# Turning the softmax maxima of each attention head: one VectorE block transpose and four ScalarE copies instead of four TensorE transposes and one copy

## The reference, cut to what matters

```python
y_dca, y_main = y[:, -16:, :], y[:, :-16, :]
q = _ln((x @ Wq + bq).reshape(b, s1, H, HD), qn_w, qn_b)      # H = 16, HD = 32
k, v = _ln(key half of y_main, kn_w, kn_b), value half of y_main
ctx = softmax(q k^T * HD ** -0.5) v
ctx = ctx + softmax(q k_dca^T * HD ** -0.5) v_dca
x = x + ctx @ Wo + bo
# then layer norm, a router with the top 6 of 64 experts, SwiGLU experts, a shared expert
```

## Time and profile before

| | |
|---|---|
| median of three runs | 1738.54 us (1735.64, 1738.54, 1740.47) |
| profiled execution, own time | 1737.14 us |
| its span | 1735.4 us |
| TensorE busy (matmul) | 1675.9 us, 97% of the span, 11782 instructions |
| VectorE busy | 1089.4 us, 63%, 2159 instructions |
| ScalarE busy | 1030.7 us, 59%, 1875 instructions |
| GpSimd busy | 769.1 us, 44%, 719 instructions |
| heads stage | about 77 to 600 us of the span |

### The profile page before, as it was taken

How to read it: one execution, slowest core, us unless ns; L and a number is a source line. 1 busy time by engine, 2 the same in 40 slices (tenths; PEclk the granted TensorE clock), 3 DMA queues, 4 the chain that set the end, 5 groups by cost and what they waited for, 6 DMA issues and landing times.

```text
span 1735.4 us, 35874 instructions
## 1 busy us (share of the span) xinstructions
PE 1675.9 (97%) x11782; PEld 1534.1 (88%) x11782; DVE 1089.4 (63%) x2159; ACT 1030.7 (59%) x1875; POOL 769.1 (44%) x719
## 2 busy tenths in 40 slices
PE   4799999999999999999999999999999999999996
PEld 3588888888888889999999999999999999999995
DVE  7555656777677665434666666666666666666665
ACT  4567766666646452223666666666666666666665
POOL 6523222334323330351355555555555555555554
PEclk9999999999999999999999999999999999999998
DMA  5543433433322532313577777778777777777775
GB/s 191 169 118 88 126 101 98 122 84 104 94 81 80 180 110 100 112 38 128 184 220 214 219 230 220 208 213 228 225 211 206 225 225 214 215 223 220 227 210 168
DMA packets 148634, 287.71 MB, mean 166 GB/s; under 512 B 29230, under 2 KB 66350, under 8 KB 139328
## 3 DMA queue, kind: packets, MB, share of 16 engines
q1 hardware_dynamic: 115584, 236.05, 42.0%
q0 software_dynamic: 32960, 50.51, 14.0%
HBM read 241.83 MB, written 64.52 MB: 177 GB/s over the span
## 4 chain that ended last, share of the span: by engine, by line
PE 88%; ACT 3%; issue 3%; DVE 2%; POOL 1%; DMA 1%; POOLq 1%; DVEq 0%; ACTq 0%; SPq 0%
PE ps L2490 37%; PE ps L2508 19%; PE ps L1470 8%; PE ps L1478 5%; PE ps L1451 4%; PE ps L2467 4%; PE ps L1441 3%; PE ps L1467 2%; PE ps L1493 2%; PE ps L1426 1%; PE ps L2485 1%; PE ps L2831 1%; ACT prob L1138 1%; DMA raw_gu<-in_w_gu 1%; ACT L1138 0%
## 5 line engine op out<-in xcount | busy, mean ns | idle before, releaser
L2217 POOL DMA_INDIRECT out<-y,ids_s x128 | 206.5, 1613 | 301.8 <-issue 162.6
L2490 PE MATMUL ps<-xt_hi,gu_hi 128*128 128x256 f32 (+1 forms) x1856 | 303.0, 285 | 0.6 <-issue 0.6
L2490 PE MATMUL ps<-xt_lo,gu_hi 128*128 128x256 f32 (+1 forms) x1856 | 290.3, 278 | 0.0
L2490 PE MATMUL ps<-xt_hi,gu_lo 128*128 128x256 f32 (+1 forms) x1856 | 289.6, 278 | 0.0
L2256 DVE TENSOR_TENSOR gu_lo<-raw_gu,gu_hi 128x1408 fp32r<-128x1408 f32 (+2 forms) x132 | 214.6, 1626 | 112.4 <-ACT gu_hi L2253 112.3
L1138 ACT ACTIVATE prob<-ps 128x512 f32<-128x512 f32 x256 | 152.3, 597 | 183.0 <-PE ps L1451 180.4
L2490 PEld LDWEIGHTS ps<-xt_hi,gu_hi 128*128 128x128 f32 (+1 forms) x1856 | 251.4, 181 | 7.6 <-issue 0.9
L2490 PEld LDWEIGHTS ps<-xt_lo,gu_hi 128*128 128x128 f32 (+1 forms) x1856 | 244.7, 181 | 0.0
L2490 PEld LDWEIGHTS ps<-xt_hi,gu_lo 128*128 128x128 f32 (+1 forms) x1856 | 244.6, 181 | 0.0
L2197 POOL DMA_INDIRECT xg<-h_rows,ids_g x128 | 189.4, 1480 | 114.3 <-POOL ids_g L2192 50.6
L2313 ACT ACTIVATE h_hi<-h 128x256 fp32r<-128x256 f32 (+1 forms) x240 | 100.5, 419 | 222.0 <-DVE h L2382 221.9
(11 more groups left out here) (318 smaller groups left out, 3001.3 us busy)
## 6 DMA issues: line engine op xcount, KB each, us to landing
raw_gu<-in_w_gu SPq DMA_DIRECT2D x70, 1408.0 KB, 8.4
raw_d<-in_w_d SPq DMA_DIRECT2D x70, 512.0 KB, 4.1
raw_d<-in_w_d SPq DMA_DIRECT2D x70, 192.0 KB, 4.5
qs<-qk_rows SPq DMA_DIRECT2D x192, 64.0 KB, 2.0
ks<-qk_rows SPq DMA_DIRECT2D x192, 64.0 KB, 2.0
xa<-in_x SPq DMA_DIRECT2D x16, 256.0 KB, 2.9
qk_rows<-k_hi SPq DMA_DIRECT2D x16, 256.0 KB, 2.2
qk_rows<-k_lo SPq DMA_DIRECT2D x16, 256.0 KB, 2.5
```

Of the source, the lines that this page charges most:

```text
L2217: pool.indirect_dma_start(out=out, out_offset=bass.IndirectOffsetOnAxis(B.ids_s[:, p, k:k + 1], 0), in_=B.y[:, p, k, :], in_offset=None, b ...
L2490: last = pe.matmul(gu_banks(it, c)[half], gu_columns(w, it, half, d, c), x[:, x_p, d, 0:W], start=i == 0, stop=i == len(steps) - 1)
```

## The change

Before, the maxima of a head were turned by four transposes on TensorE into PSUM, and ScalarE copied 32 rows of 512 out of PSUM. Now VectorE runs one transpose instruction on the whole of `nmax` behind the maxima of a head's second half (`turn_maxima`). It transposes each 32 x 32 block in place of the block, so that in the new tile `turned_max` the rows of tokens 32a to 32a + 31 of every token tile lie on partitions 32a to 32a + 31. ScalarE gathers them with four copies, one from each group of 32 partitions, each of 32 rows by four pieces of 32 tokens, out of SBUF into `qs[96:128]`. The wait of `turn_scores(n, 0)` is for the last of the four. The four transposes of `opened(n)` go, with their waits, among them those for the router's use of the bank TRB.

```diff
+            def turn_maxima(n):
+                if not head(n):
+                    return
+                if n >= 1:
+                    dve.wait_ge(shift_ready.sem, shift_ready.value(n - 1, 1))
+                dve.transpose(turned_max[:], nmax[:, n % 2].bitcast(F32).rearrange("p t j -> p (t j)")).then_inc(turned_ready.sem, 1)
...
                 maxima(n + 1, 1)
+                turn_maxima(n + 1)
...
             def shift_rows(n):
                 if not head(n):
                     return
-                act.wait_ge(nmT_ready.sem, nmT_ready.value(n, 1))
-                act.activation(qs[96:128, n % RING, :], ps[0:32, TRB, :], ACT.Copy).then_inc(nmT_in.sem, 1)
+                act.wait_ge(turned_ready.sem, turned_ready.value(n, 1))
+                rows = qs[96:128, n % RING, :].rearrange("p (t a j) -> p t a j", t=T, j=32)
+                for a in range(P // 32):
+                    last = act.activation(rows[:, :, a, :],
+                                          turned_max[32 * a:32 * a + 32, :].rearrange("p (t j) -> p t j", j=32), ACT.Copy)
+                last.then_inc(shift_ready.sem, 1)
...
-            def shift_turned(n):
...
-                pe.wait_ge(nmax_ready.sem, nmax_ready.value(n, 2))
-                if n >= 1:
-                    pe.wait_ge(nmT_in.sem, nmT_in.value(n - 1, 1))
...
-                for t in range(T):
-                    last = pe.transpose(ps[0:32, TRB, t * P:(t + 1) * P], nmax[:, n % 2, t, :].bitcast(F32), ident[:])
-                last.then_inc(nmT_ready.sem, 1)
...
                 if c == 0:
-                    pe.wait_ge(nmT_in.sem, nmT_in.value(n, 1))
+                    pe.wait_ge(shift_ready.sem, shift_ready.value(n, 1))
...
             def opened(n):
-                shift_turned(n)
                 scores(n + 1, 0)
```

More of the change, by code:

```diff
@@ L154, in attention_phase @@
         prob = sb("prob", [P, 2, T, S])
-        nmax = sb("nmax", [P, 2, T, 32], F32R)
+        nmax, turned_max = sb("nmax", [P, 2, T, 32], F32R), sb("turned_max", [P, T * 32])
         rz = sb("rz", [P, T, 2])
@@ L219, in attention_phase @@
         score_ready, nmax_ready = sig("score_ready", 2), sig("nmax_ready", 2)
-        nmT_ready, nmT_in = sig("nmT_ready", 1), sig("nmT_in", 1)
+        turned_ready, shift_ready = sig("turned_ready", 1), sig("shift_ready", 1)
         sT_ready, prob_ready = sig("sT_ready", T), sig("prob_ready", T)
@@ L657, in maxima @@
                 dve.wait_ge(score_ready.sem, score_ready.value(n, half + 1))
-                if half == 0 and n >= 2:
-                    dve.wait_ge(nmT_ready.sem, nmT_ready.value(n - 2, 1))
                 t = slice(2 * half, 2 * half + 2)
@@ L932, in front @@
                     maxima(0, 1)
+                    turn_maxima(0)
             front_begin()
@@ L954, in heads_vector @@
                 maxima(n + 2, 1)
+                turn_maxima(n + 2)
                 if projects:
@@ L966, in heads_vector @@
                 maxima(n + 3, 1)
+                turn_maxima(n + 3)
                 take_pos(u - 6)
@@ L977, in heads_vector @@
                 maxima(n + 4, 1)
+                turn_maxima(n + 4)
                 if projects:
@@ L1413, in heads_tensor @@
         def heads_tensor(pe, net):
-            def shift_turned(n):
-                if not head(n):
-                    return
-                pe.wait_ge(nmax_ready.sem, nmax_ready.value(n, 2))
-                if n >= 1:
-                    pe.wait_ge(nmT_in.sem, nmT_in.value(n - 1, 1))
[L1420 to L1424, removed]
-                for t in range(T):
-                    last = pe.transpose(ps[0:32, TRB, t * P:(t + 1) * P], nmax[:, n % 2, t, :].bitcast(F32), ident[:])
-                last.then_inc(nmT_ready.sem, 1)
             def scores(n, half):
@@ L1781, in heads_tensor @@
             wo_half(WAIT1, 1)
-            pe.wait_ge(nmT_in.sem, nmT_in.value(HEADS - 1, 1))
             a_last(WAIT1 + 2, pos_taken, GROUP1 - 1)
```

## The result

The changed kernel takes 1846.57 us (median of four runs, 1837.61 to 1847.51) where the kernel before takes 1738.99 us beside it: a ratio of 1.061, 95% interval 1.0574 to 1.0646. It is slower by 6%, about 108 us, ten times the 11 us that were forecast and far outside the range. The direction was right; the size was not.

What follows compares the result with a forecast made beforehand. TensorE was taken to bound the heads stage, already waiting for ScalarE at some points. The profiled 1737.1 us + 7.9 for heads + 3 for the clock = 1748.0; the median lies 1.4 above, so 1749 us, range 1734 to 1758.

Steps and rivals of the forecast that it cites:

- What bounds the kernel: Heads stage: TensorE bounds it as a whole, busy 512.29 of 524.00 us, but already stands idle for ScalarE at some points.
- The prices: Per head: four ScalarE copies cost 0.64 us more, TensorE saves 0.36 us, VectorE's transpose takes 0.40 us at most, hidden.
- The first rival: ScalarE's four copies overlap, costing 0.29 us more per head instead of 0.64: about 1735.5 us; chance 0.18.
- The second: Only TensorE's busy time counts, so all 23 us of transposes are saved: about 1716 us; chance 0.05.
- The heads: Gains and losses summed over all kinds of heads: 5.8 us gained, 13.7 lost, 7.9 us slower.
- the cover: Time hiding VectorE's transpose behind other work; if gone in three fourth heads that wait for VectorE's division, 1.2 us.
- The clock: Late third heads: more TensorE idle time makes two more of six fall to 1.2 GHz, 3 us, between 0 and about 7.
- The third rival: The clock falls in most late heads, 10 × 1.4 = 14 us on top: about 1758 us; chance 0.15.

Runs made afterwards that it cites:

- kernel with filler: The changed kernel with unneeded transposes of a constant on TensorE at openings that wait and ahead of waiting turns of scores; 1749.15 us, ratio 1.0068.

## Why the prediction was wrong, point by point

**What bounds the kernel** was right: TensorE as a whole, ScalarE at the openings.

**The prices** were right. The turn on ScalarE costs 0.67 us more (0.64 forecast), the transpose on VectorE 0.31 us and hidden (0.40 at the most). The first rival, overlapping copies, is out: 1.26 us from the first to the end of the fourth. The second, 23 us saved whole, is out too.

**The heads** were nearly right: 11.5 us where 7.9 were forecast. In the kernel with filler the clock stays up, and the time from the fourth exponential of one head to that of the next, less the same in the kernel before, can be summed by kind (us, worked out from the starts of L1138 and L1152):

| heads | forecast | kernel with filler |
|---|---|---|
| 10 third, query product | −3.6 | −4.0 |
| 7 fourth, key product | −1.7 | −1.5 |
| 3 fourth, wait for VectorE | 0 | +1.2 |
| 10 first, wo_product | 0 | +0.5 |
| head 20 and heads 0, 1 | −0.5 | −0.2 |
| 6 second, a_turned (units 4 to 9) | +1.1 | +1.2 |
| 8 with a plain opening (7 early heads and head 43) | +5.1 | +6.0 |
| 11 late second and fourth | +3.7 | +4.3 |
| 6 late third | +3.8 | +4.0 (without what head 42 gains by its clock, 1.6) |
| sum | +7.9 | +11.5, and +9.8 with head 42 |

The three fourth heads are the cover that the prediction named and priced at 1.2 us at the most. The filler itself may add to some heads, but where the changed kernel's own clock is up (heads 24 to 34 and 37 to 40) its heads differ from these by 0.06 us at the most.

**The clock** is the step that failed: "I expect two more of six to fall: 3 us, between 0 and about 7". The term measured about 98 us: 256 us at 1.2 GHz in place of some 10, 246 us more, and a stretch at that level loses about 0.40 us per us (a late fourth head, 59, takes 11.29 us at the low level and 6.76 in the kernel with filler at the high one: 4.53 / 11.29). That agrees with the difference of the two medians, 1846.6 − 1749.2 = 97 us, and 98 with the 9.8 of the heads makes the 108 us measured. Three things in the step were wrong:

- *Where.* It looked at the late third heads only, and judged by the length of one wait: 0.66 us went ahead of a fall and 0.48 did not the earlier trace rows. The changed kernel's clock falls thirteen times. Seven falls lie before 508 us: one in head 0, as before; three in early heads, behind a wait of 0.86 us for the copies; one in head 35, behind 0.80 us for VectorE's division; and two in heads 41 and 43. The six from 508 us on stand behind an opening with two gaps of 0.20 to 0.23 us (as in the fence on head 53), and five of these were plain second or fourth heads. For these heads the prediction did write down the wait and the lateness (0.22 and 0.35 us), as time; it did not ask what they do to the clock.
- *How long.* It took the stretch of the earlier trace rows for the length of a fall: 0.57 over 4 us is 3.4 us at 1.2 GHz (not "about half the time", though the 1.7 us lost do follow from 0.57). The thirteen stretches after the change last 3.4 to 41 us, 20 on the mean, so that a fall costs about 8 us and not 1.4 to 1.7; and yet TensorE hardly waits in the long ones (busy 33.63 of 34.00 us).
- *What makes it.* It counted added waiting for the copies. The removed transposes count as well: where a head is bound by ScalarE, 0.36 us less work is 0.36 us more idle time. With one copy and no transposes, the copy is only 0.04 us slower and 139 us are still at the low level.

The trace of the kernel before already held a stretch longer than that of the earlier trace rows, about 10 us in head 0, of which these are two windows:

```profile
82.00:84.00 2.00, 2.00 (x6) 0.98 (x4) 0.76 (x1) 1.60 (x2) 0.00 (x0) 0.50 0.61 127
...
86.00:88.00 2.00, 2.00 (x9) 1.45 (x8) 1.88 (x4) 1.31 (x4) 0.00 (x0) 0.50 0.89 263
```

The third rival had the mechanism and nearly the number of falls; its price (10 × 1.4 us) failed by the length, and it, too, looked at the late heads only.

That TensorE's idle places are the cause is shown by the filler, which changes nothing but TensorE's work in them and gives 97 us back, and by VectorE's transpose alone, which costs nothing. The filler takes away idle time and adds work at once; which of the two the clock answers to, these runs can't tell. The Trainium skill (TensorE: Matmul & The Clock Gate, section "A second HAM failure mode: psum-queue depth-cycling") tells of short idle gaps between groups of matmuls that make the clock swing between its two levels; the runs here agree (gaps of 0.20 to 1.1 us, thirteen falls). How much idle time it takes, and why a low stretch lasts as long as it does, the runs leave open: an opening at 556 us in the changed kernel has the same two gaps (0.22 and 0.20 us) and no fall behind it.

## What to carry to other kernels

Where TensorE is nearly always busy, as here, its work in a place that waits for another engine can cost nothing and keep the clock up; before taking it out, find the heads that wait and price the clock over whole stretches, not over the wait. A change that pays in the places with slack should be made there and nowhere else: on 12 of 64 heads this one gains 0.3%, on all of them it loses 6%. Where idle time can't be avoided, work that nobody needs can be the cheapest repair, tested by one run.

## What was not expected of the hardware

- Two gaps of 0.2 us in one head, all the idle time of the 10 us before, went ahead of 34 us at 1.2 GHz (from 587.3), and one of 1.12 us ahead of 10 us (336 us, the change on 20 heads).
- The same kernel without its useless filler is 97 us slower, with the same work on every other engine.
- Four small ScalarE copies from different partitions follow each other without overlap, 1.26 us for 4 × 0.307, whereas four longer ones on the same partitions did overlap.
